# TensorE multiplies a constant matrix, into banks that nobody reads, while it waits in the opening and at the changes of stage

## The chip, the cores and the metric

One core of one Trainium2 chip runs the whole program. The metric is the device time of one execution in microseconds; less is better. TensorE has two clock levels, 1.2 and 2.4 GHz; the profile shows the granted level of each stretch as 0.50 or 1.00.

## The reference, cut to what matters

Two layers, each a gated cross attention and a gated mixture of experts, over x (8 batches of 100 tokens of 512) and a context (8 batches of 722 rows of 512):

```python
x = x + tanh(g_xattn[0]) * perceiver_attention(ctx, layernorm(x), mask)      # 16 heads, keys = 722 context rows + 100 latents
x = x + tanh(g_ffn[0])   * experts(layernorm(x), 4 experts, best 2)
x = x + tanh(g_xattn[1]) * strided_attention(layernorm(x), ctx, stride 16)   # 16 heads, 45 keys each
x = x + tanh(g_ffn[1])   * experts(layernorm(x), 8 experts, best 2)
```

## The kernel before

The program runs four stages one after the other, each with a block for every engine and a barrier of all engines between them. Names in the profile carry the stage's letter: `a_` perceiver attention (0 to 985 us), `f_` the first expert stage (to 1510), `g_` the strided attention (to 1650; `ahead_` and `sums_` name tensors that it shares with stage f), `m_` the second expert stage (to the end). Instructions of one engine are issued in the order in which they are written, and semaphores tie the engines together; no planner reorders anything.

**Stage a, opening.** VectorE normalises the first four batches of latents (line 1051). TensorE turns them (`turn_latents(0)`, line 843), and then makes the queries of all heads in sixteen units (`queries(u)`, line 703): four fp32 products of 128x400 each, which the profile counts as eight instructions a unit. The first unit waits for the weights `wq_sb` from DRAM. ScalarE and VectorE split each unit into a high and a low part (lines 540 and 946), split the weights (586 and 1026) and the context rows (533 and 935). `keys(0, 0)` waits for fifteen low parts of the queries and for the split context, the first scores (line 759) for the low part of the first keys (line 951), which stands behind four splits of `wv` (line 1026) in VectorE's order.

**Stage a, end.** After the last attention, TensorE routes batch 6 (`route_next(B - 2)`, line 822), waits for VectorE to normalise batch 7 (line 1014), turns it (`turn_next(B - 1)`, line 807), waits for ScalarE to move it (line 575), and routes it. VectorE keeps the logits (line 1021), SyncE waits for its last stores, and the barrier follows.

**Expert stages, opening.** On POOL: constants. TensorE multiplies them into an index vector (lines 1643, 1644), and when VectorE has chosen the experts (line 1782), counts the tokens of each (1648, 1649). VectorE computes from the counts which token goes to which row, some 35 small operations. When it has written the expert of each slot (line 1813), TensorE's sequencer reads the first six of them into registers (`expert_of`, line 1653, `EARLY` = 6). When VectorE has written `at_row` (line 1836, two halves), sixteen products (line 1662) gather the row numbers. The sequencer reads the other expert numbers (eight in f, ten in m) meanwhile. VectorE, which has split four weight pieces in the meantime (line 1843), takes the row numbers over (line 1849); POOL starts the gathers (line 1548); when the first has landed, VectorE goes on with the other splits, the low parts of the tokens (line 1857) and the gates (lines 1903 to 1909), and TensorE turns the tokens (`turn_tokens`, line 1674) and makes the first hidden layer (`hidden`, lines 1161 to 1163).

**Stage g, opening.** TensorE projects four pieces of the context (`context(c)`, line 2358), each when it has landed, and turns the tokens (`tokens(b)`, line 2366) as VectorE normalises them (line 2516); then queries, for which the weights must be split.

Of the kernel before, what the change touches and what calls it, by code (L numbers as in the profile page):

```python
# [58 lines left out]
def perceiver_attention(nc, ctx_rows, ctx_cols, x_in, keep_mask, ln_cols, wq, wkv, wout,  # L59
# [7 lines left out]
    P = 128  # L67
# [29 lines left out]
    with ExitStack() as ctx:  # L97
# [54 lines left out]
        ident = sb("ident", [P, P])  # L152
        stats = sb("stats", [P, CT + 2, 6])
        mean_var = sb("mean_var", [P, CT + 2, 2])
        unread = sb("unread", [P, 2 * B + 2])
# [17 lines left out]
        kv_ps = ps("kv_ps", [P, 2, BANK])  # L173
        s_ps = ps("s_ps", [P, 2, 2 * BANK])
        t_ps = ps("t_ps", [P, BANK])
# [16 lines left out]
        const_done = sem("const_done")  # L192
# [16 lines left out]
        l_norm_done = sem("l_norm_done")  # L209
# [469 lines left out]
        def _(pe):  # L679
# [14 lines left out]
            def queries(u):  # L694
                h, m = divmod(u, PAIRS)
                pe.wait_ge(lat_t_done, KD * (h + 1))
                pe.wait_ge(wq_loaded, 16)
                if Q_RING[u][0] == "s":
                    pe.wait_ge(lat_t_done, 2 * KD)
                if q_before(u) is not None:  # L700
                    pe.wait_ge(q_lo_done, q_before(u) + 1)
                for k in range(KD):
                    ins = nc.tensor.matmul(q_bank(u)[:, 0:HM], wq_sb[:, k, P * m:P * m + P], lat_t[:, k, HM * h:HM * h + HM], start=(k == 0), stop=(k == KD - 1))
                ins.then_inc(q_ready, 1)
# [105 lines left out]
            def route_next(b):  # L810
                if b == 0:
                    pe.wait_ge(ahead.loaded, 16 * ahead.loads)
                if b == B - 1:
                    wait_read(pe, ("turn", b))
                else:
                    pe.wait_ge(o_free, o_use["turn", b] + 1)
                if b >= B - 2:
                    wait_kv("route", b)
                else:
                    wait_o("route", b)  # L820
                for k in range(KD):
                    ins = nc.tensor.matmul(route_bank(b)[0:M, 0:ahead.experts], xn_t[:, k, :], ahead.r_t[:, k, :], start=(k == 0), stop=(k == KD - 1))
                ins.then_inc(routed, 1)
# [12 lines left out]
            def turn_latents(h):  # L836
                pe.wait_ge(l_norm_done, HB * (h + 1))
                for k in range(KD):
                    u = KD * h + k
                    if u >= 4:  # L840
                        pe.wait_ge(lat_t_done, u - 3)
                    for j in range(HB):
                        ins = nc.tensor.transpose(l_bank(u)[:, M * j:M * j + M], lat[0:M, HB * h + j, P * k:P * k + P], ident[0:M, 0:M])
                    ins.then_inc(l_tr_done, 1)

            pe.wait_ge(const_done, 3)
            turn_latents(0)
            queries(0)
            queries(1)
            turn_latents(1)  # L850
# [40 lines left out]
            attend(n)  # L891
            finish_last(7)
            route_next(B - 2)
            turn_next(B - 1)
            route_next(B - 1)

        @block.vector
        def _(dve):
# [309 lines left out]
def gated_experts(nc, name, x_in, routing, pieces, gate, gates, y_pairs, x_out, core, tensors=None, ahead=None, handed=None):  # L1208
# [29 lines left out]
    with ExitStack() as ctx:  # L1238
# [400 lines left out]

        @block.tensor  # L1640
        def _(pe):
            pe.wait_ge(const_done, 5)
            nc.tensor.matmul(banks[:, CONST, 0:P], ones, earlier, start=True, stop=True)
            nc.tensor.matmul(banks[:, CONST, P:P + 1], earlier, ones[:, 0:1], start=True, stop=True).then_inc(iota_ready, 1)

            pe.wait_ge(chosen_done, 1)
            flat = "p b e -> p (b e)"
            nc.tensor.matmul(banks[:, POS, B * E:2 * B * E], ones[0:M, :], chosen[0:M, :, :].rearrange(flat), start=True, stop=True).then_inc(count_ready, 1)
            nc.tensor.matmul(banks[0:M, POS, 0:B * E], earlier[0:M, 0:M], chosen[0:M, :, :].rearrange(flat), start=True, stop=True).then_inc(count_ready, 1)
            pe.wait_ge(expert_done, 1)  # L1650

            def expert_of(n):
                return pe.value_load(expert[0:1, n:n + 1], min_val=0, max_val=E - 1)
# [2 lines left out]
                return [expert_of(FIRST[q] + s) for s in range(SIZE[q])]  # L1656

            slot_expert = [expert_of(s) for s in range(EARLY)]
            for i in range(B * TOP):
                if i % B == 0:  # L1660
                    pe.wait_ge(at_row_done, i // B + 1)
                ins = nc.tensor.matmul(banks[:, CONST, 0:2 * SLOTS], at_row[0:M, i, :], in_slot[0:M, i, :, :].rearrange("p t s -> p (t s)"),  # L1662
                                       start=(i == 0), stop=(i == B * TOP - 1))
            ins.then_inc(rows_ready, 1)
            slot_expert += [expert_of(s) for s in range(EARLY, CORE)]

            pe.wait_ge(const_done, 12)

# [81 lines left out]

            first_group(0, True, slot_expert)
            other_groups(0, slot_expert)
            pe.wait_ge(expert_done, 2)
            used = pe.value_load(expert[0:1, SLOTS:SLOTS + 1], min_val=0, max_val=SLOTS)
            with pe.If(used > CORE):
# [279 lines left out]
def strided_attention(nc, x_in, y_pairs, gates, ahead, sums, wq_t, bias_qkv, wo_t, bo, gate, x_out, routing):  # L2035
# [22 lines left out]
    with ExitStack() as ctx:  # L2058
# [285 lines left out]
        def _(pe):  # L2344
# [34 lines left out]
            def half(h):  # L2379
                for b in range(HB * h, HB * h + HB):  # L2380
                    pe.wait_ge(fill_free("x", b), bank_use["x", b] // 4 + 1)
                for n in range(KD * h, KD * h + KD):
                    queries(n)

            context(0)
            pe.wait_ge(const_done, 3)
            for b in range(HB):
                tokens(b)
            context(1)
            pe.wait_ge(wq_lo_done, KD)  # L2390
            half(0)
# [329 lines left out]
```

## Time and profile before

| | us |
|---|---|
| median of 3 runs | 2014.9 (2014.32 to 2020.66) |
| the profiled execution, its own time | 2010.7 |
| its span, first to last instruction | 2009.0 |
| TensorE busy | 1886.8 (94% of the span) |
| VectorE, ScalarE, POOL busy | 1006.6, 858.4, 639.8 |
| mean granted clock of TensorE | 0.971 |

Times in the rows below are counted from the start of the span. A row of TensorE's busy time says how long matmuls were in flight; an fp32 product is two instructions, an fp32r product or a turning one.

### The profile page before, as it was taken

How to read it: one execution, taken by the hardware profiler on the slowest of the kernel's cores; microseconds unless marked ns; L12 is line 12 of the kernel's file. 1: busy time of each engine (PE TensorE's matmuls, PEld its weight loads, DVE VectorE, ACT ScalarE, POOL GpSimd, SP SyncE). 2: the span in 40 equal slices, each digit the busy share in tenths (PEclk: the TensorE clock that was granted, in tenths of full speed). 3: DMA queues.
4: the chain of work that ended last, by engine and by line, in shares of the span. 5: the costliest groups of instructions: out<-in, count | busy, mean ns of one | idle time of the engine just before them, and what ended most of it. 6: DMA issues, size and time to landing. Idle time of an engine off the chain costs nothing. (4 is left out here: it accounts for less than half of the span.)

```text
span 2009.0 us, 35165 instructions
## 1 busy us (share of the span) xinstructions
PE 1886.8 (94%) x12136; PEld 1539.5 (77%) x12136; DVE 1006.6 (50%) x2225; ACT 858.4 (43%) x1796; POOL 639.8 (32%) x519
## 2 busy tenths in 40 slices
PE   6999999999999999999599999999997876999994
PEld 3688787887878787878478888888884766999984
DVE  5526564655555554535553333233345657544565
ACT  3334453544444444435443334233323535655650
POOL 1230201102030302000045554355521204787882
PEclk9999999999999999999789999999998987999997
DMA  8840112121121211000343333133358035645546
GB/s 234 302 135 23 55 39 81 39 81 39 55 64 55 63 41 42 9 27 13 108 121 110 111 115 125 46 111 111 119 202 306 9 98 181 193 154 168 209 147 216
DMA packets 105398, 218.84 MB, mean 109 GB/s; under 512 B 25295, under 2 KB 26095, under 8 KB 103323
## 3 DMA queue, kind: packets, MB, share of 16 engines
q1 hardware_dynamic: 100451, 201.21, 31.2%
q0 software_dynamic: 4800, 15.73, 2.3%
q8 instruction: 85, 1.39, 0.3%
q14 instruction: 62, 0.51, 0.1%
HBM read 188.46 MB, written 28.04 MB: 108 GB/s over the span
## 5 line engine op out<-in xcount | busy, mean ns | idle before, releaser
L501 POOL TENSOR_TENSOR a_kvin_raw<-a_kvin_raw,a_rows 128x722 f32<-128x722 f32 x32 | 57.0, 1782 | 555.9 <-DMA a_rows<-a_norm_dram 555.9
L682 PE MATMUL a_kv_ps<-a_kvin_hi,a_wk_hi 128*128 128x512 f32 (+1 forms) x512 | 190.4, 372 | 0.0
L1161 PE MATMUL f_banks<-f_wab_hi,f_x_hi 128*128 x448 | 183.8, 410 | 1.1 <-DVE f_x_lo L1857 1.1
L684 PE MATMUL a_kv_ps<-a_kvin_hi,a_wk_lo 128*128 128x512 f32 (+1 forms) x512 | 179.7, 351 | 0.0
L683 PE MATMUL a_kv_ps<-a_kvin_lo,a_wk_hi 128*128 128x512 f32 (+1 forms) x512 | 178.9, 350 | 0.0
L1163 PE MATMUL f_banks<-f_wab_hi,f_x_lo 128*128 x448 | 176.8, 395 | 0.0
L1162 PE MATMUL f_banks<-f_wab_lo,f_x_hi 128*128 x448 | 176.2, 393 | 0.0
L1602 ACT ACTIVATE f_h_sb<-f_banks 128x256 f32<-128x256 f32 x112 | 43.1, 385 | 292.9 <-PE f_banks L1163 292.9
L1879 DVE TENSOR_TENSOR f_h_sb<-f_h_sb,f_banks 128x256 f32<-128x256 f32 x112 | 47.2, 422 | 240.8 <-ACT f_h_sb L1602 239.4
L569 ACT ACTIVATE a_probs_t<-a_t_ps 128x500 f32<-128x500 f32 x128 | 74.9, 585 | 190.8 <-PE a_t_ps L773 190.8
L1161 PE MATMUL m_banks<-m_wab_hi,m_x_hi 128*128 x512 | 154.0, 301 | 1.6 <-DVE m_x_lo L1857 0.9
L682 PE MATMUL a_kv_ps<-a_wv_hi,a_kvin_hi 128*128 128x512 f32 (+1 forms) x384 | 152.3, 397 | 0.0
L684 PE MATMUL a_kv_ps<-a_wv_hi,a_kvin_lo 128*128 128x512 f32 (+1 forms) x384 | 151.8, 395 | 0.0
L579 ACT ACTIVATE a_probs<-a_probs,a_neg_max 100x822 f32<-100x822 f32 x128 | 125.4, 979 | 61.3 <-DVE a_neg_max L958 61.2
L683 PE MATMUL a_kv_ps<-a_wv_lo,a_kvin_hi 128*128 128x512 f32 (+1 forms) x384 | 151.5, 394 | 0.0
L1163 PE MATMUL m_banks<-m_wab_hi,m_x_lo 128*128 x512 | 145.4, 284 | 0.0
L1162 PE MATMUL m_banks<-m_wab_lo,m_x_hi 128*128 x512 | 145.0, 283 | 0.0
L958 DVE CUSTOM_DVE_ANT_0 a_probs<-a_s_ps,a_mask_add 100x822 f32<-100x822 f32 x128 | 128.6, 1004 | 1.4 <-PE a_s_ps L759 1.2
L1540 POOL TENSOR_TENSOR f_wy_lo<-f_raw,f_wy_hi 128x512 fp32r<-128x512 f32 x60 | 77.3, 1289 | 157.7 <-ACT f_wy_hi L1579 157.7
L562 ACT ACTIVATE a_k_hi<-a_kv_ps 128x512 fp32r<-128x512 f32 (+1 forms) x128 | 65.6, 514 | 105.6 <-PE a_kv_ps L684 105.6
L551 ACT ACTIVATE a_v_sb<-a_kv_ps 128x512 f32<-128x512 f32 x96 | 57.1, 595 | 123.6 <-PE a_kv_ps L684 123.6
L1540 POOL TENSOR_TENSOR m_wab_lo<-m_wab_raw,m_wab_hi 128x512 fp32r<-128x512 f32 x84 | 108.2, 1328 | 0.0
(423 smaller groups left out, 4791.8 us busy)
## 6 DMA issues: line engine op xcount, KB each, us to landing
f_raw<-f_pieces SPq DMA_DIRECT2D x94, 256.0 KB, 2.6
m_raw<-m_pieces SPq DMA_DIRECT2D x92, 256.0 KB, 3.0
f_wab_raw<-f_pieces SPq DMA_DIRECT2D x42, 512.0 KB, 5.9
m_wab_raw<-m_pieces SPq DMA_DIRECT2D x42, 512.0 KB, 6.0
a_kvin_raw<-a_ctx_t SPq DMA_DIRECT2D x8, 1444.0 KB, 8.1
a_rows<-ctx SPq DMA_DIRECT2D x8, 1440.0 KB
a_rows<-a_norm_dram SPq DMA_DIRECT2D x8, 722.0 KB, 5.4
ahead_piece<-g_ctx SPq DMA_DIRECT2D x2, 2880.0 KB, 19.9
```

Of the source, the lines that this page charges most:

```text
L551: nc.scalar.activation(v_sb[0:n, half, t, :], kv_bank("v", i, v)[0:n, 0:HALF], ACT.Copy).then_inc(kv_sem("v", i, v), 1)
L562: nc.scalar.activation(k_hi[:, c:c + w], kv_bank("k", n, part)[:, 0:w], ACT.Copy).then_inc(k_hi_done, 1)
L569: nc.scalar.activation(probs_t[:, x, M * a:M * b], turned_bank(x, 0), ACT.Copy).then_inc(ta_done, 1)
L579: nc.scalar.activation(probs[0:M, x, 0:KEYS], probs[0:M, x, 0:KEYS], ACT.Exp, scale=-1.0, bias=neg_max[0:M, x:x + 1], accum_out=row_sum[0: ...
L682: nc.tensor.matmul(out, hi_l, hi_r, start=first, stop=False)
L683: nc.tensor.matmul(out, hi_l, lo_r, start=False, stop=False)
L684: return nc.tensor.matmul(out, lo_l, hi_r, start=False, stop=last)
L958: nc.vector.tensor_tensor_reduce(out=probs[0:M, x, 0:KEYS], in0=s_ps[0:M, x, 0:KEYS], in1=mask_add[0:M, :], scale=-1.0, scalar=3.0e38, op0 ...
L1161: nc.tensor.matmul(out, left_hi, right_hi, start=start, stop=False)
L1162: nc.tensor.matmul(out, left_hi, right_lo, start=False, stop=False)
L1163: return nc.tensor.matmul(out, left_lo, right_hi, start=False, stop=stop)
L1540: nc.gpsimd.tensor_tensor(split_dst(wab_lo, wy_lo, c), raw_of(q, n), split_dst(wab_hi, wy_hi, c).bitcast(F32), ALU.subtract).then_inc(wlo_ ...
```

## The change

119 products are added to TensorE's stream. Each multiplies a 128x128 fp32 constant (the identity, or a matrix of ones in the expert stages) by itself into a PSUM bank whose content nobody reads. They carry no semaphore. Nothing is removed or moved; three waits are added ahead of products in places where TensorE would have waited a little later anyhow (for the first latents, for the first normalised batch, and for POOL's constants).

In numbers: 27 in the opening of a, 13 at its end, 30 in the opening of f, 4 at its end, 15 in the opening of g, 30 in the opening of m.

```diff
+            def unread(n, bank):
+                for _ in range(n):
+                    nc.tensor.matmul(bank[:, 0:P], ident[:, :], ident[:, :], start=True, stop=True)
+
             pe.wait_ge(const_done, 3)
+            unread(10, kv_ps[:, 0, :])
+            pe.wait_ge(l_loaded[0], 16)
+            unread(12, kv_ps[:, 0, :])
+            pe.wait_ge(l_norm_done, 1)
+            unread(2, kv_ps[:, 0, :])
             turn_latents(0)
+            unread(3, kv_ps[:, 0, :])
             queries(0)
...
             finish_last(7)
             route_next(B - 2)
+            unread(9, t_ps)
             turn_next(B - 1)
+            unread(2, t_ps)
             route_next(B - 1)
+            unread(2, t_ps)
...
+            def unread(n, of):
+                for _ in range(n):
+                    nc.tensor.matmul(banks[:, HT_T, 0:P], of, of, start=True, stop=True)
+
+            pe.wait_ge(const_done, 3)
+            unread(1, ones)
             pe.wait_ge(const_done, 5)
             nc.tensor.matmul(banks[:, CONST, 0:P], ones, earlier, start=True, stop=True)
             nc.tensor.matmul(banks[:, CONST, P:P + 1], earlier, ones[:, 0:1], start=True, stop=True).then_inc(iota_ready, 1)
+            unread(2, ones)
...
             nc.tensor.matmul(banks[0:M, POS, 0:B * E], earlier[0:M, 0:M], chosen[0:M, :, :].rearrange(flat), start=True, stop=True).then_inc(count_ready, 1)
+            unread(10, ones)
             pe.wait_ge(expert_done, 1)
...
             slot_expert = [expert_of(s) for s in range(EARLY)]
+            unread(11, ones)
             for i in range(B * TOP):
...
             slot_expert += [expert_of(s) for s in range(EARLY, CORE)]
+            unread(6, ones)
...
             other_groups(0, slot_expert)
+            if x_out is None:
+                unread(4, ident[:, :])
...
             context(0)
             pe.wait_ge(const_done, 3)
+            unread(10)
             for b in range(HB):
                 tokens(b)
+                if b == 1:
+                    unread(5)
             context(1)
```

## Rows read from the trace of the kernel before

**Rows 1.** The span and TensorE's mean granted clock, by core.
```profile
core 0: 2009.0 us, clock 0.971
```

**Rows 2.** Stretches: length, busy time of PE, PEld, DVE, ACT, POOL; granted clock; DMA share; GB/s.
```profile
78.70:976.70 898.00, 895.83 (x6418) 717.27 (x6416) 468.32 (x1065) 396.91 (x715) 111.50 (x65) 1.00 0.18 55
...
989.40:997.40 8.00, 0.00 (x0) 0.00 (x0) 7.21 (x30) 6.87 (x12) 0.00 (x0) 0.50 1.02 378
...
1018.40:1507.30 488.90, 488.88 (x2255) 398.03 (x2254) 170.65 (x349) 174.85 (x409) 231.19 (x187) 1.00 0.34 114
...
1577.90:1588.60 10.70, 8.29 (x80) 7.27 (x80) 8.76 (x12) 5.31 (x11) 4.72 (x4) 0.84 0.01 2
```

**Rows 3.** Timeline of TensorE in the opening: start, duration, engine, line, count, idle before.
```profile
22.64 5.67 PE L703 MATMUL a_t_ps<-a_lat_t,a_wq_sb 128*128 128x400 f32 x8 [4.84 <-DMA a_wq_sb<-L_xattn_Wq]
28.11 2.98 PE L703 MATMUL a_o_ps<-a_lat_t,a_wq_sb 128*128 128x400 f32 x8
...
77.39 0.47 PE L759 MATMUL a_s_ps<-a_k_hi,a_q_hi 64*100 64x512 f32 x2 [2.77 <-DVE a_k_lo L951]
```

**Rows 4.** Timeline of VectorE ahead of the first scores.
```profile
68.82 0.56 DVE L946 SCALAR_TENSOR_TENSOR a_qs_lo<-a_kv_ps,a_qs_hi 128x400 fp32r<-128x400 f32 x1
...
71.62 4.63 DVE L1026 TENSOR_TENSOR a_wv_lo<-a_wout_sb,a_wv_hi 128x1024 fp32r<-128x1024 f32 x4 [0.37 <-ACT a_wv_hi L586]
```

**Rows 5.** Timeline of TensorE at the end of stage a.
```profile
975.88 0.79 PE L822 MATMUL a_kv_ps<-f_ahead_r_t,a_xn_t 128*100 128x4 f32 x8
981.31 0.93 PE L807 MATMUL a_kv_ps<-a_ident,a_res 100*128 100x100 f32 x4 [4.64 <-DVE a_res L1014]
982.83 1.49 PE L822 MATMUL a_kv_ps<-f_ahead_r_t,a_xn_t 128*100 128x4 f32 x8 [0.59 <-ACT a_xn_t L575]
```

**Rows 6.** SyncE's waits, 960 to 990 us: total, times, longest.
```profile
SPq L480 <- DMA f_xn<-a_res: 2.2, 1, 2.2
```

**Rows 7.** Timelines of SyncE's queue and of VectorE at the end of stage a.
```profile
981.28 0.27 SPq L403 DMA_DIRECT2D f_xn<-a_res  x1
...
984.36 0.16 DVE L1021 TENSOR_TENSOR logits<-a_kv_ps,f_ahead_r_bias 100x4 f32<-100x4 f32 x1 [3.11 <-PE a_kv_ps L822]
```

**Rows 8.** Register loads of TensorE's sequencer, f: duration ns min/median/max, first and last start.
```profile
L1653 PEldq SEQ_ASSERT  x6: 18/18/28, 993.5 to 996.7; - x6
...
L1653 PEldq TENSOR_LOAD <-f_expert x8: 295/300/308, 998.6 to 1003.1; - x8
```

**Rows 9.** The same in stage m, first six.
```profile
L1653 PEldq SEQ_ASSERT  x6: 18/18/18, 1660.9 to 1664.2; - x6
```

**Rows 10.** Timeline of TensorE in the opening of f.
```profile
986.89 0.80 PE L1643 MATMUL f_banks<-f_scratch 128*128 128x128 f32 x2 [2.56 <-POOL f_scratch L1528]
...
997.46 3.60 PE L1662 MATMUL f_banks<-f_in_slot,f_at_row 100*128 100x32 f32 x16 [8.07 <-DVE f_at_row L1836]
...
1018.42 0.49 PE L1161 MATMUL f_banks<-f_wab_hi,f_x_hi 128*128 x1
```

**Rows 11.** Timeline of VectorE in the opening of f.
```profile
998.46 2.49 DVE L1843 TENSOR_TENSOR f_wab_lo<-f_y_acc,f_wab_hi 128x512 fp32r<-128x512 f32 x4
...
1005.28 2.54 DVE L1843 TENSOR_TENSOR f_wab_lo<-f_y_acc,f_wab_hi 128x512 fp32r<-128x512 f32 x4 [3.67 <-DMA f_y_acc<-f_xn,f_rows_at]
...
1017.39 0.68 DVE L1857 TENSOR_TENSOR f_x_lo<-f_banks,f_x_hi 128x512 fp32r<-128x512 f32 x1
```

**Rows 12.** The chain of work that ended last, in the opening of m.
```profile
1665.64 3.62 PE m_banks L1662 x16
...
1669.73 3.26 DMA m_y_acc<-m_xn,m_rows_at
```

**Rows 13.** Timeline of TensorE in the opening of g.
```profile
1510.58 5.03 PE L2358 MATMUL g_banks<-ahead_piece,ahead_wk 128*32 128x360 f32 x32 [3.30 <-PEq L2657]
...
1523.66 1.57 PE L2366 MATMUL g_banks<-g_ident,sums_y_got 100*128 100x100 f32 x8 [5.08 <-DVE sums_y_got L2516]
...
1546.01 2.63 PE L2358 MATMUL g_banks<-ahead_piece,ahead_wk 128*32 128x360 f32 x32 [0.64 <-DMA ahead_piece<-g_ctx]
```

More of the change, by code:

```diff
@@ L2383, in half, with unread @@
                     queries(n)
+            def unread(n):
+                for _ in range(n):
+                    nc.tensor.matmul(banks[:, Y, 0:P], ident[:, :], ident[:, :], start=True, stop=True)
             context(0)
             pe.wait_ge(const_done, 3)
+            unread(10)
             for b in range(HB):
                 tokens(b)
+                if b == 1:
+                    unread(5)
             context(1)
```

## The prediction

> **What bounds the kernel now.** I read four views in this order. The clock by core comes first [rows 1]: 0.971 over 2009.0 us. With two levels, 1.00 and 0.50, that is (1 - 0.971) x 2009.0 / 0.5 = 117 us at the low one. The table of stretches says where not: in the long middle of stage a and in nearly all of f, TensorE is busy for 895.83 of 898.00 us and for 488.88 of 488.90, at 1.00 [rows 2]. There TensorE is the bound, and a microsecond that a stage's opening gains or loses goes through to the end. The low level lies at the changes of stage, and there TensorE mostly waits: in 989.4 to 997.4 it is busy for 0.00 us, and VectorE for 7.21 [rows 2]. The timelines then show what ends each wait, and what is late next; in the openings it is a DMA or VectorE. In the opening I go by durations: the same eight instructions take 5.67 us at 22.64 and 2.98 at 28.11 [rows 3]. The first unit ran at the low level.
>
> So the change can only gain where TensorE's work at the low level ends last, and it can lose where a filler stands in front of real work that is ready.
>
> **What one filler costs.** It is an fp32 product of 128 columns, two instructions. The query units have 400 columns: (28.11 - 22.64) / 4 = 1.37 us a product at the low level, 2.69 / 4 = 0.67 at the full one (2.98 less the 0.3 in which the last one drains) [rows 3]. By columns, 128 / 400 of that is 0.44 and 0.21 us. The nearest row of the form itself is 0.80 us for one product at the low level, from start to drained [rows 10]; behind one another they overlap, so I take 0.43 and 0.21, and 0.15 more for the first of a sequence.
>
> **Opening of a (27 fillers).** They end before what they stand in front of. The last three follow the turned latents, some 18 us, and take 1.3 us at most; the queries start at 22.64, when their weights land [rows 3]. So they cost nothing, and 3.5 to 5.5 us without work remain ahead of the queries. In this trace the level was low after 4.64 us of idling [rows 5], after 3.30 and after 5.08 [rows 13], and still full after 2.77 (two 64x512 products in 0.47) [rows 3]. I take the low level, gain 0. The other bound: with the first unit at full level TensorE is 2.7 us ahead. But the fifteenth low part of the queries is done at 68.82 + 0.56 = 69.4 whatever TensorE does, since VectorE is then working through a queue; the sixteenth then ends near 69.9 and not at 71.25, and the four splits, 4.63 us, and the keys' low part, which end the wait of 2.77 at 77.39, can start 1.7 us earlier [rows 3, 4]. Gain 0 to 1.7.
>
> **End of a (13).** Nine fillers fill 1.9 of the 4.64 us ahead of the turning [rows 5], leaving 2.7; by the same rows the level rather holds. Then turning ends 0.4 us earlier, routing takes 0.79 instead of 1.49, together 1.1 [rows 5]. The barrier needs the store as well: SyncE has issued it at 981.55 and waits 2.2 us, so to 983.75, while VectorE's last operation ends at 984.52 [rows 6, 7]. Gain 0.75. If the level is low, the two fillers behind the last routing (0.85 us) end at 984.32 + 0.85 = 985.2, a loss of 0.65. I take the gain.
>
> **Openings of f and m (30 each).** Here I expect the sum to be made. Three fillers go around the constants; two of them can hold the counts up for 0.4 us at the low level. I take 0, because VectorE has other small operations to do ahead of reading the counts, and keep 0.4 as the bound. Ten follow the counts at 989.4 and run to 991.5 or 993.8. The six register loads follow when VectorE has written the experts, one each 0.64 us, and end at 996.7 [rows 8]. They are the sequencer's, and the eight further ones from 998.6 run beside the sixteen products that end at 1001.06 [rows 8, 10], so loads and products don't wait for each other, only for their turn in the stream. The eleven fillers thus start at 996.7, and the sixteen products behind them, which started at 997.46, must wait for all eleven. TensorE has idled for 3 to 5 us by then: low level, as above.
> - Low to the end: 996.7 + 0.15 + 11 x 0.43 = 1001.6, and 3.6 us of products [rows 10] end at 1005.2 instead of 1001.06: 4.1 late.
> - Lifted on the way, at the soonest: in the rows the level rose 5.5 us after work began at 22.64 [rows 3]; the shortest low spell in stage g, with TensorE at work through most of it, lasted 10.70 x (1 - 0.84) / 0.5 = 3.4 us [rows 2], and I take that as the lower bound. Then eight fillers are low and three full: 996.85 + 3.4 + 0.65 = 1000.9, the sixteen at half their time 1.8, to 1002.7: 1.6 late.
> - Full from the start: 996.85 + 2.3 + 1.8 = 1000.95, no gain, since VectorE splits until 1000.95 and only then takes the rows over [rows 11].
>
> I take the middle of the first two, 2.9. Nothing hides it: the gathers wait for those rows, VectorE for the gathers (1005.28), and from there its queue runs to the low part at 1017.39 to 1018.07 that lets TensorE go on at 1018.42 [rows 10, 11]. For the same reason what the full level gives to the turning and first hidden layers in between (some 3 us of TensorE) is worth nothing. The last six fillers start near 1003.8 and end by 1006.5, before the shifted landing at 1006.9 or later.
>
> In m the loads end at 1664.2 and the sixteen started at 1665.64 [rows 9, 12]. Low to the end: 1664.2 + 0.15 + 4.7 + 3.6 = 1672.7 instead of 1669.26, 3.4 late. Lifted: 1664.35 + 3.4 + 0.65 + 1.8 = 1670.2, 0.9 late. Full: nothing. I take 2.2. The six last fillers start near 1673.2, after the landing at 1673.0 [rows 12]; at the low level they hold the tokens for up to 2.5 us, of which the first four splits (2.5 us) and the shift hide most: 0 to 1, I take 0.
>
> A rule of the Trainium skill speaks against this part too: "TensorE: Matmul & The Clock Gate", What happens when you issue a matmul, has weight loads pulled ahead of matmuls in flight, and the matmuls themselves kept in program order. By it the eleven can't be overtaken, which is the 1.6 to 4.1 above; if the queue let ready products pass, f and m would cost 0. No row of before shows either, since no ready product stands behind another there.
>
> **End of f and opening of g (4 and 15).** The four take 1.0 us of the 3.30 to the barrier [rows 13]. In g, ten end before 1523.66 even at the low level, and five (2.2 us) go into a later wait for VectorE's tokens; were they a few tenths late, the third piece would hide it. What the full level could give (some 4 us on two pieces of context) ends at the third piece: TensorE waits for its DMA at 1546.01 already [rows 13]. Zero, both ways, but for a shift of a few tenths.
>
> **The sum.** 0 - 0.75 + 2.9 + 2.2 = +4.35 us on 2010.7, the profiled execution's own time (1.7 above its span): 2015.0. The median of the runs, 2014.9, is 4.2 above that execution; the same shift makes 2019.2.
>
> **The rivals.** *Kept level:* the fillers do hold the clock at 1.00, at least at the eleven. Against: 3 to 5 us of idling that the loads force. For: 21 of the fillers lie within 12 us. Then f and m cost nothing: -0.75, and -1.7 with the opening: 2012.5 to 2014.2, and 2013.8 as its centre. It ends on the other side; the point that decides is the duration of the first of the eleven, 0.43 or 0.21. *One late:* one of f and m lifts or keeps, the other doesn't: about +1.5, 2016.5. *All of it paid:* TensorE's work at the low level is on the path after all, and half of its time comes back: 2.7 + 1.1 in a, 1.8 and some 3 in f, 2.5 (of 5.03) and some 2 in g, 1.8 and some 2 in m [rows 3, 5, 10, 12, 13], 17 us: 1998. Against: every wait that I followed there ends in VectorE or a DMA. A rule would make even more of it: the page named above, under Terms, puts the penalty at the throttled time times one minus the level; by it the sum would be 117 x 0.5 = 58 us less. The trace does not agree: TensorE was busy in 0.00 of the 8.00 us of one such stretch. *Nothing happens:* the fillers change neither level nor rows; within 0.5 us of 2014.9.
>
> **How the numbers follow.** Late rows in f and m: 0.55. One late: 0.13. Kept: 0.14. All paid, or much of it: 0.08. Nothing: 0.10. The low bound takes in the kept level, 2012.0. The high one is both losses in full, 4.1 + 3.4 - 0.75 and the last six, +7.5: 2022.5. What a measurement of this kernel can tell from no change is 0.3%, 6 us. The likeliest case passes it only at its upper end, about a third of the time: slower 0.20, faster 0.09, within 0.71.
>
> **What would show it.** The sixteen products start near 1001 instead of 997.5 and last 1.8 to 3.6 us; VectorE waits for them and takes the rows over 1.6 to 4.1 us later, and likewise in m. The queries at 22.64 still take 5.5 us. At the end of a the turning lasts 0.5 and the barrier comes 0.75 earlier. It would be wrong if the eleven took 0.21 each, or if the six register loads no longer ended at 996.7, since then the gap ahead of the sixteen moves.

## The result, and the profile after

The changed kernel took 2023.9 us (median of 14 runs, 2019.9 to 2030.6), the kernel before 2016.0 us beside it (median of 14, 2012.3 to 2020.7): ratio 1.0037, 95% interval 1.0027 to 1.0047, so 5.4 to 9.5 us slower. The forecast was 2019.2 us, within 2012.0 to 2022.5: the sign of the sum was right, its size too small, and the time lies outside the range. The profiled execution took 2019.9 us, span 2018.1, 9.1 more than the span before.

Clock of the one core, the counterpart of [rows 1]:

```profile
core 0: 2018.1 us, clock 0.974
```

The clock rose, from 0.971 to 0.974, and the kernel became slower. The rise isn't only this execution's. Averaged over their runs, six of the seven kernels of the experiments with fillers in the openings of both f and m lie 0.002 to 0.004 above the kernel before beside them (0.969 to 0.972 against 0.966 to 0.968); the three with fillers in a alone lie at 0.966 to 0.967, no higher than before. So the fillers of the expert stages do raise the clock a little, and what they buy was not on the path. TensorE in the opening of f, the counterpart of [rows 10] (start, duration, line, count, idle before and what ended it):

```profile
988.25 4.61 PE L1657 MATMUL f_banks<-f_scratch 128*128 128x128 f32 x20
995.67 4.01 PE L1657 MATMUL f_banks<-f_scratch 128*128 128x128 f32 x22 [2.80 <-issue]
999.33 2.38 PE L1684 MATMUL f_banks<-f_in_slot,f_at_row 100*128 100x32 f32 x16
1004.19 2.92 PE L1657 MATMUL f_banks<-f_scratch 128*128 128x128 f32 x12 [2.49 <-issue]
1006.91 1.13 PE L1697 MATMUL f_banks<-f_ident,f_y_acc 128*128 128x128 f32 x8
```

Line 1657 is the filler; two instructions are one filler. The third row is what VectorE waits for (1.92 us, until 1001.74). The same place in m:

```profile
1660.14 4.58 PE L1657 MATMUL m_banks<-m_scratch 128*128 128x128 f32 x20
1668.08 4.90 PE L1657 MATMUL m_banks<-m_scratch 128*128 128x128 f32 x22 [3.35 <-issue]
1672.73 1.94 PE L1684 MATMUL m_banks<-m_in_slot,m_at_row 100*128 100x40 f32 x16
1678.97 2.93 PE L1657 MATMUL m_banks<-m_scratch 128*128 128x128 f32 x12 [4.29 <-issue]
1681.69 1.65 PE L1697 MATMUL m_banks<-m_ident,m_y_acc 128*128 128x128 f32 x8
```

The fourth and fifth rows are the place that I had taken for free: the turning starts when the six fillers are through, not when the tokens land (1678.43, the next fence's first row), and VectorE then has nothing to do for 2.45 us:

```profile
1678.43 2.54 DVE L1868 TENSOR_TENSOR m_wab_lo<-m_y_acc,m_wab_hi 128x512 fp32r<-128x512 f32 x4 [3.19 <-DMA m_y_acc<-m_xn,m_rows_at]
1683.42 0.69 DVE L1882 TENSOR_TENSOR m_x_lo<-m_banks,m_x_hi 128x512 fp32r<-128x512 f32 x1 [2.45 <-ACT m_x_hi L1602]
```

Before, with the same columns, it had no gap at all between the two, and the turning stood 0.29 us behind the landing. The third row is ScalarE's high part, on which the low part waits:

```profile
1673.01 2.54 DVE L1843 TENSOR_TENSOR m_wab_lo<-m_y_acc,m_wab_hi 128x512 fp32r<-128x512 f32 x4 [3.21 <-DMA m_y_acc<-m_xn,m_rows_at]
1673.30 2.29 PE L1674 MATMUL m_banks<-m_ident,m_y_acc 128*128 128x128 f32 x8 [4.06 <-DMA m_y_acc<-m_xn,m_rows_at]
1674.42 0.60 ACT L1589 ACTIVATE m_x_hi<-m_banks 128x512 fp32r<-128x512 f32 x1 [6.21 <-PE m_banks L1674]
1675.47 0.68 DVE L1857 TENSOR_TENSOR m_x_lo<-m_banks,m_x_hi 128x512 fp32r<-128x512 f32 x1
```

TensorE's waits in the changed kernel, 975 to 2018 us (total, times, longest):

```profile
PE m_banks L1711 <- DVE m_h_sb L1904: 8.1, 5, 4.0
PE m_banks L1657 <- issue: 7.6, 2, 4.3
...
PE f_banks L1657 <- issue: 5.3, 2, 2.8
```

"Issue" ahead of a filler is the register loads: nothing that the fillers waited for, but what stood ahead of them in the stream. The first row is the longest wait behind the opening of m: TensorE waits up to 4.0 us for VectorE, where it waited 2.4.

Since single executions differ by chance (see the last section), I read every trace by stretches between two events that only the work between them can move. Worked out from the timelines, in us:

| stretch | before | after | difference |
|---|---|---|---|
| start to the first scores of a | 77.39 | 76.89 | -0.50 |
| to the barrier of f | 908.50 | 907.87 | -0.63 |
| to VectorE taking over the rows in f | 15.21 | 16.98 | +1.77 |
| to the last product of f | 505.79 | 505.80 | 0.01 |
| to SyncE's first load of y in g | 5.06 | 6.38 | +1.32 |
| to the third piece of context | 34.06 | 35.56 | +1.50 |
| to the constants' product in m | 106.53 | 106.88 | +0.35 |
| to VectorE taking over the rows in m | 16.74 | 18.35 | +1.61 |
| to the first gated `h_sb` of m | 15.04 | 17.52 | +2.48 |
| to the end | 324.68 | 325.87 | +1.19 |

### The profile page after: what moved, and what is told of

It is laid out like the page before. It is cut to its first block and busy times, and to the rows that moved or that the text cites. A ratio compares the mean times of both kernels' runs of the same rounds, so it can differ in the third digit from the quotient of the medians.

```text
span 2018.1 us, 35639 instructions
## 1 busy us (share of the span) xinstructions
PE 1919.9 (95%) x12374; PEld 1574.6 (78%) x12374; DVE 1006.4 (50%) x2225; ACT 858.5 (43%) x1796; POOL 640.0 (32%) x519
```

## The experiments

Twelve kernels in four groups, each group timed beside the kernel before on one chip: medians of before 2015.7 (experiments 1 to 4), 2016.6 (5 to 8), 2025.4 (9 to 11), 2015.1 (12). Differences are ratio minus one, times 2016, with the 95% interval. An interval is some 6 us wide, wider than most questions asked; the medians say how much a kernel costs in all, the stretches of the traces say where. There is one trace of each kernel, fourteen with the two above. "Landing" is the time from which the first gathered tokens are there, read from the start of VectorE's split that waits for them; "rows" is the time at which VectorE takes the row numbers over; "the sixteen" are the products that gather them.

### 1. Without the eleven

```diff
             slot_expert = [expert_of(s) for s in range(EARLY)]
-            unread(11, ones)
             for i in range(B * TOP):
```

> The changed kernel without the eleven unread products ahead of the sixteen row products, in both expert stages; all other fillers stay. Theory (queueing): in f and m nothing but the register loads stands ahead of the sixteen products, so they start within 0.5 us of VectorE's first half of at_row, as before the change, and VectorE takes the rows over when its own four splits are done: 1.8 us earlier than in the changed kernel in f, 1.6 us in m. Of the +7.5 us of the medians about +4 remain, because the six fillers behind the second register loads still hold the tokens of m for 2.4 us. Rival (the eleven are the whole price, as my sum had it): the time falls back to the kernel before, within 1 us.

Ratio 1.0033 (1.0020 to 1.0045): +6.7 us (4.0 to 9.1). In the trace VectorE takes the rows over 14.97 us behind the barrier of f and 16.74 behind the constants of m: 2.0 and 1.6 us less than in the changed kernel, to the hundredth the time of before in m. The sixteen wait for `at_row` again, and the six still hold the tokens:

```profile
1671.08 3.60 PE L1683 MATMUL m_banks<-m_in_slot,m_at_row 100*128 100x40 f32 x16 [4.74 <-DVE m_at_row L1860]
1678.67 2.92 PE L1657 MATMUL m_banks<-m_scratch 128*128 128x128 f32 x12 [4.00 <-issue]
1681.39 1.91 PE L1696 MATMUL m_banks<-m_ident,m_y_acc 128*128 128x128 f32 x8
```

The rival, that the eleven are the whole price, falls. But I had expected about +4 to remain, and the median fell by 0.8 us only, from +7.5 to +6.7; the interval just reaches down to 4.0. That the eleven cost 1.6 to 2.0 us a stage is read from the stretches; the times alone don't show it.

### 2. Without the six, in m alone

```diff
-            unread(6, ones)
+            if x_out is None:
+                unread(6, ones)
```

> The changed kernel without the six unread products behind the second register loads, in stage m alone. Theory: the loads of the ten expert numbers end after the tokens have landed, the six fillers stand behind the loads and the turning of the tokens behind the fillers; without them the turning starts at the end of the loads, VectorE's first low part of the tokens 2.5 us earlier against the landing, the later wait for m_h_sb shrinks from 4.0 us to about 2.4 and the group behind it stays at full level: 2.5 to 3.7 us less than the changed kernel, about +4 to +5 against the kernel before. Rival (VectorE's four splits cover the six, as predicted): the same time as the changed kernel, +7.5.

Ratio 1.0022 (1.0007 to 1.0037): +4.4 us (1.4 to 7.5), the profiled execution 3.2 below the changed kernel's. From the landing to the first gated `h_sb` 11.31 us, as before (11.31; changed kernel 13.80), and the wait behind it is 2.2 us instead of 4.0:

```profile
1679.43 2.16 PE L1698 MATMUL m_banks<-m_ident,m_y_acc 128*128 128x128 f32 x8 [4.35 <-DMA m_y_acc<-m_xn,m_rows_at]
```

```profile
PE m_banks L1712 <- DVE m_h_sb L1905: 6.3, 5, 2.2
```

That the splits cover the six, which I had predicted, is wrong. The times alone would not have told it, since the intervals of this kernel and of the changed one overlap; the stretch does.

### 3. The six ahead of the second loads

```diff
-            slot_expert += [expert_of(s) for s in range(EARLY, CORE)]
             unread(6, ones)
+            slot_expert += [expert_of(s) for s in range(EARLY, CORE)]
```

> The changed kernel with the six unread products moved ahead of the second register loads, in both expert stages: same number of fillers, other place. Theory (it is the place behind the loads that costs): they run directly behind the sixteen products while the sequencer reads the registers, and the tokens are turned at the end of the loads; the same gain as taking them out of m, 2.5 to 3.7 us below the changed kernel. Rival (the six cost wherever they stand, for example by moving the loads behind them): the ten loads start later by the time of six products, 1.3 to 2.6 us, and nothing is gained.

Ratio 1.0037 (1.0023 to 1.0051): +7.5 us. Half of each theory: the turning starts 2.02 us behind the landing (changed kernel 3.26, without the six 0.46), and the stretch to `h_sb` takes 12.58 us (13.80 and 11.31).

```profile
1675.34 1.94 PE L1684 MATMUL m_banks<-m_in_slot,m_at_row 100*128 100x40 f32 x16
1677.12 1.59 PE L1657 MATMUL m_banks<-m_scratch 128*128 128x128 f32 x12
1683.03 1.94 PE L1697 MATMUL m_banks<-m_ident,m_y_acc 128*128 128x128 f32 x8 [4.32 <-issue]
```

The ten loads ran from 1676.5 to 1683.0. In the changed kernel they began 0.2 us ahead of the sixteen, here 1.2 us behind their start, when some 10 of the 16 were through, so that about 6 of them and the 12 instructions of the fillers were still to run. So fillers ahead of loads aren't free: they hold the loads up as soon as the sequencer is some 17 instructions ahead (see the last section).

### 4. Twelve instead of six, in m

```diff
-            unread(6, ones)
+            unread(6 if x_out is None else 12, ones)
```

> The changed kernel with twelve instead of six unread products behind the second register loads of m. Theory: each further filler delays the tokens by its own duration, 0.42 us at the low level and 0.21 at the full one; in the changed kernel the level rose while the six ran or just after, so six more cost 1.3 to 2.5 us: +9 to +10 against the kernel before, and the turning starts that much later behind the landing. Rival (hidden by VectorE's splits): unchanged, +7.5.

Ratio 1.0054 (1.0033 to 1.0074): +10.9 us (6.7 to 14.9), 3.4 above the changed kernel, where +1.3 to +2.5 was expected. The trace gives the dose:

```profile
1685.47 5.43 PE L1657 MATMUL m_banks<-m_scratch 128*128 128x128 f32 x24 [3.68 <-issue]
1690.73 1.04 PE L1697 MATMUL m_banks<-m_ident,m_y_acc 128*128 128x128 f32 x8
```

Twelve take 5.43 us, six took 2.93; from the constants' product to the turning it is 27.84 us, against 25.33 with six and 22.66 with none: 2.7 us for the first six, 2.5 for the second. Behind the landing it shows less, 15.26 us to `h_sb` against 13.80, because the rows, and with them the landing, were 0.6 us later in this trace.

### 5, 6 and 9. One region at a time

The changed kernel with only the fillers of a (40), only those around the barrier between f and g (19), only those of the expert openings (60).

> Only the fillers of stage a (27 in the opening, 13 at its end); nothing is added in f, g and m. Theory: the end of a gains 0.6 us from its last attention to the barrier and nothing else changes: 2 us at most below the kernel before, within what can be told from no change. f, g and m then have the same durations from milestone to milestone as before the change, and g's first load of y is issued 5.1 us after the last product of f, not 5.7 to 6.6 as in the four runs with fillers there. Rival (the extra loss of 1.2 us at the head of g and the 1.5 us in the landing of its third piece are chance or come from elsewhere): the same 5.7 to 6.6 here.

> Only the four fillers at the end of f and the fifteen in the opening of g. Theory (as in the prediction, they lie beside DMAs): the first product of g comes 0.4 us later behind the last of f (4.07 instead of 3.69 us, which five traces showed), the rest nothing: within 1 us of the kernel before. Rival (the fillers at the end of f or in g cost what the changed kernel lost there in its profiled execution): +2.5 us, with the load of y issued 6 to 6.5 us behind the last product of f and the third piece 35.5 us behind that.

> Only the 30 fillers in the opening of f and the 30 in that of m; none in a, at the end of f and in g. Theory: these alone make the change slower. From the barrier to VectorE's taking over of the rows +1.4 to +2.4 us in f (0.34 of them ahead of the counts) and +1.6 in m, from the landing in m to the first gated h_sb +2.5, and up to 1.2 behind it: +6 to +7.5 us in all, and the load of y in g issued 4.4 to 5.3 us behind the last product of f, as in the five traces without this pair of places together. Rival (the fillers around f's end and in g are needed for the loss, though alone they cost nothing): +4 or less.

| kept | ratio | us |
|---|---|---|
| a | 1.0000 (0.9985 to 1.0014) | 0 (-3 to +3) |
| end of f and g | 1.0000 (0.9986 to 1.0015) | 0 (-3 to +3) |
| openings of f and m | 1.0027 (1.0014 to 1.0040) | +5.4 (2.8 to 8.1) |

The loss is made in the expert openings; their interval reaches down to 2.8, so the times don't exclude the rival (that the nineteen are needed for a part of it, +4 or less). There, alone, barrier to rows took 16.99 us in f, constants to rows 18.27 in m, landing to turning 3.21: the changed kernel's numbers. From the landing to `h_sb` it was 16.12, more than the changed kernel's 13.80: VectorE idled 3.06 us ahead of it, where it idled 0.80 before, and ScalarE's `h_sb`, for which the profile names no wait, came late too. No filler stands there; the cause is open. The end of a didn't gain in experiment 5: from the sixth batch's routing to the barrier it took 10.36 us with its thirteen fillers, against 10.01 before. With the nineteen alone (experiment 6), the first product of g came 4.41 us behind the last of f (3.69 or 3.70 in all seven traces without them) and the third piece 39.94 us behind it (38.3 to 39.5 in those seven). Their interval of 3 us would hide the 2.5 of the rival; it is the trace that speaks against it, with the load of y 4.66 us behind the last product of f and not 6 to 6.5.

### 7. Ten behind the turned latents

```diff
             turn_latents(0)
-            unread(3, kv_ps[:, 0, :])
+            unread(10, kv_ps[:, 0, :])
             queries(0)
```

(f, g and m as before.)

> As the kernel with only the fillers of a, but ten instead of three of them behind the turned latents, so that TensorE's idling ahead of the queries is under 2 us instead of 3.8. Theory: the level rises on the way and holds, the first unit of queries takes 3.0 us instead of 5.4, and what follows is bounded as the prediction says: the first scores come up to 1.7 us earlier. Rival 1: the level falls again and the fillers, still at the low level, end behind the landing of the weights, so that the queries start up to 1 us late. Rival 2: the first unit is fast, but the first scores don't come earlier, as VectorE's queue ends last: 0.

Ratio 0.9993 (0.9977 to 1.0009). The ten ran at the full level, so they were over in 2.42 us, 3.97 us of idling remained, and the queries ran at the low one, 5.67 us, so that the first scores came 54.80 us behind their start, as before (54.75). My bridge was too short by my own price list: I had sized it at the low level.

### 8. The eleven ahead of the first loads, no six

```diff
-            unread(10, ones)
+            unread(21, ones)
             pe.wait_ge(expert_done, 1)
...
             slot_expert = [expert_of(s) for s in range(EARLY)]
-            unread(11, ones)
...
-            unread(6, ones)
```

(a as changed; nothing at the end of f and in g.)

> Expert stages with the eleven fillers moved ahead of the first six register loads (21 in a row behind the counts), the six behind the second loads left out; a as in the changed kernel, none at the end of f and in g. Theory: a sequencer runs only some 11 to 15 products ahead of its engine (in three traces the ten register loads of m began 2.0 to 2.5 us before the last product ahead of them ended), so the 21 push the loads by about 1.3 us in m, but the sixteen row products start at most 0.5 us later than VectorE's first half of at_row would let them: f and m cost 0 to 0.5 us each instead of 1.7 and 1.6 plus 2.5; the whole is -1.5 to +1 us against the kernel before. Rival (fillers delay by their own time wherever they stand in the queue): +1.6 in each of f and m, about +3 in all.

Ratio 0.9996 (0.9982 to 1.0010): -0.8 us. Barrier to rows in f 14.97 us (15.21 before), constants to rows in m 16.52 (16.74), landing to `h_sb` 11.31. Nothing unread stands in front of ready work any more:

```profile
1659.64 7.64 PE L1657 MATMUL m_banks<-m_scratch 128*128 128x128 f32 x42
1668.96 2.21 PE L1683 MATMUL m_banks<-m_in_slot,m_at_row 100*128 100x40 f32 x16 [1.68 <-DVE m_at_row L1857]
1676.68 2.05 PE L1695 MATMUL m_banks<-m_ident,m_y_acc 128*128 128x128 f32 x8 [5.51 <-DMA m_y_acc<-m_xn,m_rows_at]
```

The same 21 fillers, ahead of the loads instead of astride of them, cost nothing: the rival (their own time wherever they stand) falls. The expectation's "11 to 15 products ahead" was worked out from traces in which the sequencer had waited for `at_row`; where it hadn't, it is some 17 (experiment 3).

### 10. Nothing but the six of m

```diff
             slot_expert += [expert_of(s) for s in range(EARLY, CORE)]
+            if x_out is not None:
+                unread(6, ones)
```

> The kernel before with nothing but six unread products behind the ten register loads of m. Theory: the price of the place by itself. The loads end as the tokens land (0.3 us apart before the change), TensorE has idled for 4 us and the level is low: the turning starts 6 x 0.43 = 2.6 us later, and VectorE's first low part of the tokens comes 2.3 to 2.6 us later behind the landing, with nothing that makes up for it: +2.3 to +3.7 us. Rival (it needs the eleven before it, which push the loads): under 1 us.

Ratio 1.0012 (0.9997 to 1.0028): +2.4 us (-0.6 to +5.6); landing to turning 2.90 us (0.29 before), to the first low part of the tokens 4.62 (2.46): +2.16, to `h_sb` 13.97 (11.31): +2.66. Of the last, 0.43 is idling of VectorE just ahead of `h_sb` (1.23 us, 0.80 before) that no filler explains.

```profile
1676.08 2.93 PE L1648 MATMUL m_banks<-m_scratch 128*128 128x128 f32 x12 [3.98 <-issue]
1678.80 1.50 PE L1684 MATMUL m_banks<-m_ident,m_y_acc 128*128 128x128 f32 x8
```

Six products that nobody reads, alone, cost 2.2 to 2.7 us in this trace; the interval of the times still touches no change. It doesn't need the eleven.

### 11. The version that the stretches point to

Stage a alone, with 24 behind the turned latents and none behind the last routing.

```diff
             turn_latents(0)
-            unread(3, kv_ps[:, 0, :])
+            unread(24, kv_ps[:, 0, :])
...
             route_next(B - 1)
-            unread(2, t_ps)
```

> The version that the stretches point to: stage a alone, with 24 fillers instead of three behind the turned latents, and without the two behind the last routing. Theory: at the full level the 24 take 5.8 us and end within 1 us ahead of the weights' landing; then the first unit of queries takes 2.9 us, and as the first scores came 49.0 to 49.1 us plus the first unit's own duration behind its start in six traces, they come 1.5 to 2.7 us earlier than the 54.75 of before. The barrier comes 0 to 0.6 us earlier and never later, since nothing unread stands ahead of it. In all -1.5 to -3.3 us. Rival 1: the level is low while they run, they take 10 us, the queries start some 4 us late and the kernel is 2 to 4 us slower. Rival 2: VectorE's queue takes over as the bound at 1.3 us, the most that those six traces showed.

Ratio 0.9989 (0.9975 to 1.0003): -2.2 us (-5.0 to +0.6). In the trace:

```profile
16.70 7.10 PE L848 MATMUL a_kv_ps<-a_ident 128*128 128x128 f32 x48
23.64 2.85 PE L703 MATMUL a_t_ps<-a_lat_t,a_wq_sb 128*128 128x400 f32 x8
```

The first unit takes 2.85 us, and the first scores come at 75.48, 51.84 us behind its start (54.75 before); neither rival holds as it was put. Counted from the start of the program they are 1.9 us earlier, not 2.9, because the fillers took 7.10 us and not 5.8, and ended about 1.1 us behind the time at which the queries start elsewhere (22.1 to 22.8 in twelve traces, 23.59 in experiment 4). Some 20 of them might do better; that wasn't tried. The end of a took 10.01 us, as before. This is the fastest version tried, and its interval still touches no change.

### 12. Without the four at the end of f

```diff
-            if x_out is None:
-                unread(4, ident[:, :])
```

> The changed kernel without the four fillers at the end of f; all others stay. Five traces with all the places filled show SyncE's first load of y in g 5.7 to 6.6 us behind the last product of f, eight others, among them one with these four but without those of the expert openings, 4.35 to 5.3. Theory: the barrier comes 0.3 to 0.4 us earlier, as in every trace without the four, and no more is theirs: the load of y keeps 5.3 to 6.2 us. Rival: the four are behind the whole delay, and it falls to 4.35 to 5.3. Against the kernel before +5.5 to +7.5 us either way; the trace decides, not the median.

Ratio 1.0056 (1.0040 to 1.0073), from 6 runs: +11.3 us (8.1 to 14.7), more than the changed kernel and more than the 5.5 to 7.5 expected, which the edit does not explain. The one trace speaks against my theory: first product of g back to 3.70 us behind the last of f, the load of y at 5.23, within the rival's 4.35 to 5.3. So the delay of about 1.2 us goes with the four; but alone with those of g they left it at 4.66 (experiment 6). Why is open, and one trace of each kernel doesn't exclude chance. The trace also shows the eleven at the low level to the end:

```profile
1672.57 5.06 PE L1657 MATMUL m_banks<-m_scratch 128*128 128x128 f32 x22 [3.74 <-issue]
1677.28 3.58 PE L1684 MATMUL m_banks<-m_in_slot,m_at_row 100*128 100x40 f32 x16
```

## Why the prediction was wrong, point by point

**Price of a filler: right.** 4.90 / 11 = 0.45 and 4.58 / 10 = 0.46 us at the low level, 2.42 / 10 = 0.24 at the full one; predicted 0.43 and 0.21, and 0.15 for the first.

**Opening of a: gain 0, bound 1.7. VectorE's queue isn't as fixed as I had it.** In all fourteen traces the first scores come 49.0 to 49.2 us plus the duration of the first unit behind the queries' start. So what the unit gained arrived in full, 1.3 us in experiment 5 and 2.8 in experiment 11, where I had VectorE's queue cut the gain at 1.7. I had taken the fifteenth low part to be done at 69.4 whatever TensorE does; in experiment 11 it was done at 68.26. But there the queries started 1.0 us later than before, and in experiment 5, where they started at 22.44, VectorE worked without a gap right up to its splits, so nothing was left there. Whether more than 1.3 us would arrive with queries that start on time is not shown. That the changed kernel gains little is right for the other reason given: 3.80 us of idling ahead of the queries, which took 5.37 us (4.75 to 5.67 without the fillers, 4.33 to 5.57 with the 27).

**End of a: -0.75, bound +0.65. Both happen.** From the sixth routing to the barrier it was 10.01 or 10.02 us in four traces without the fillers. With the thirteen it was 9.41, 9.41 and 9.53 where the level held through the last routing, and 10.10 to 10.67 in the six others, where the two fillers behind it stood ahead of the barrier. The mean of the nine is 10.12, a loss of 0.1. The changed kernel's profile happened to be of the first kind:

```profile
980.78 0.56 PE L807 MATMUL a_kv_ps<-a_ident,a_res 100*128 100x100 f32 x4 [2.53 <-DVE a_res L1027]
981.94 0.87 PE L822 MATMUL a_kv_ps<-f_ahead_r_t,a_xn_t 128*100 128x4 f32 x8
```

**Opening of f, +2.9; of m, the eleven, +2.2: mechanism right, somewhat too large.** The loads end 10.91 us behind the barrier (10.81 predicted), the eleven start there and the sixteen behind them. Barrier to rows in f rose by 1.6 to 2.5 us in six traces; the two fillers ahead of the counts make TensorE 0.34 us later with them, but VectorE reads them 4.12 us behind the barrier in all fourteen traces, so they cost the 0 that I had put. Constants to rows in m by 1.5 to 1.6 in four traces, 2.2 in one and 3.3 in experiment 12, which is my "low to the end" (3.4). Experiments 1 and 8 remove it from the stretches.

The Trainium skill ("TensorE: Matmul & The Clock Gate", What happens when you issue a matmul) has matmuls keep program order; the traces agree: the turning started at 1681.69, behind the six, though its tokens had landed at 1678.43.

**The six of m, 0 (0 to 1): this step failed, it is +2.5.** The prediction said: "they hold the tokens for up to 2.5 us, of which the first four splits (2.5 us) and the shift hide most". The 2.5 us that they hold them was right (2.7). The cover was not: I set the delay against the length of the work beside it, and not against what was left of it. During those same four splits (2.46 us) the turning of the first tokens and ScalarE's high part have to be done as well, and they take 2.0 of it. The slack measured: 3.26 - 0.29 = 2.97 us more from the landing to the turning gave 2.53 more to the low part, so 0.44 us was hidden; 1.73 gave 1.32 (experiment 3), so 0.41. And the shift hides nothing, because the same fillers cause it: the ten loads moved with the rows (their end at 1673.1 before and 1678.97 after, the landing at 1673.01 and 1678.43).

In f the same six cost nothing in this trace: it has eight loads, not ten, and these ended 1.8 us ahead of the landing, so the turning was 0.95 us late and landing to low part stayed at 2.46 us. In other traces of f they cost up to 0.96.

**Behind the opening of m: 1.2 us here, which I can't put down to the fillers.** The two groups of TensorE behind the turning, now at the full level, are done sooner, VectorE is later, the wait becomes 4.0 instead of 2.4 us, and the group behind it runs at the low level, 0.21 us from product to product instead of the 0.12 of the group at 1684.48. From the first product of `h_sb` to the next it takes 4.24 us, where it took 2.86 before:

```profile
1692.58 0.33 PE L1711 MATMUL m_banks<-m_ident,m_h_sb 128*128 128x128 f32 x1 [3.99 <-DVE m_h_sb L1904]
...
1693.84 0.42 PE L1175 MATMUL m_banks<-m_wab_lo,m_x_hi 128*128 x1
1694.06 0.41 PE L1176 MATMUL m_banks<-m_wab_hi,m_x_lo 128*128 x1
```

That looks like a higher level earlier that bought a lower one later, and without the six (experiment 2) the group is back at 2.86 us and the stretch at 324.62. But the kernels of experiments 5, 6 and 7, which have no filler in m and waited 1.6 us there, show the same group at the low level, for 4.40 us each, and last stretches of 326.5 to 327.8 us; with the six and a wait of 2.5 us (experiment 1) it took 2.86. From experiment 5:

```profile
1683.17 0.33 PE L1705 MATMUL m_banks<-m_ident,m_h_sb 128*128 128x128 f32 x1 [1.59 <-DVE m_h_sb L1896]
...
1684.37 0.42 PE L1175 MATMUL m_banks<-m_wab_lo,m_x_hi 128*128 x1
1684.59 0.41 PE L1176 MATMUL m_banks<-m_wab_hi,m_x_lo 128*128 x1
```

So the level of this group differs between traces with and without fillers, and the 1.2 us are a difference between two executions until more of them are compared.

**End of f and opening of g, 0 and 0: +0.34 measured at the barrier, and 2.5 us more whose cause is open.** The first product of g comes 0.3 to 0.7 us later in all six traces that have the four: TensorE was not so early at the barrier that they fit in. From the last product of f to the third piece of g the seven traces without any of the nineteen took 38.3 to 39.5 us, the five with all fillers 40.2 to 41.9. Part is the later load of y (5.06 and 6.38), the rest the landing of the third piece, which TensorE's fillers do not touch. The load of y waits for f's last scatter to land. POOL issues that scatter 1.4 us behind the last product of f in all fourteen traces; SyncE then waits for it 1.6 to 2.3 us in the five with all fillers and at most 1.3 in the nine others. Before and in the changed kernel:

```profile
SPq L2180 <- DMA y<-f_y_acc,f_rows_at: 1.1, 1, 1.1
SPq L2205 <- DMA y<-f_y_acc,f_rows_at: 2.1, 1, 2.1
```

So it is a DMA that lands later though it is issued at the same time. That it goes with the fillers is shown, not why. Alone, the nineteen measured as 0, within 3 us either way (experiment 6).

**The sum.** Predicted -0.75 + 2.9 + 2.2 = +4.35. The trace has -1.13 in a, +1.77 and +1.61 for the rows, +2.48 for the six, +1.19 behind them, +3.17 between f's last product and m (1.32 + 1.50 + 0.35): +9.09, the difference of the spans. Traced to fillers are the rows and the six, 5.86 us together; the 60 fillers of the expert openings alone cost +5.4 (experiment 9). The 1.19 and the 3.17 are not traced to them. The ratio of the runs gives 5.4 to 9.5.

Had the six been entered at the 2.5 us for which they hold the tokens, the forecast would have been +6.85 and the high bound +9.25 (2024.2), just above the measured 2023.9. The bound as it stood is a little under its own terms (4.1 + 3.4 - 0.75 + 1 = 7.75, not 7.5), and its base of 2014.9, a median of three runs, was 1.1 us below the later median of fourteen. That the middle of the measured difference, +7.5, equals the bound is chance. The rivals *kept level*, *all of it paid* and *nothing* are excluded by the ratio; *one late* by the stretches.

## What to carry to other kernels

A filler in an in-order queue is free only if everything behind it is late anyway: ask what ends each wait, and put it ahead of what ends the wait, not behind. Sequencer work (here 0.64 us a register load) moves with the queue, and here the fillers that followed it landed just where the real work became ready; the same 21 fillers cost 0 ahead of the loads and 1.6 to 1.8 us a stage astride of them. And when a delay is to be "hidden" by work beside it, subtract first what already hides there: here 2.5 us of cover had 0.4 us left.

## What the runs showed of the hardware that I had not expected

**The level is not the program's alone.** The first unit of queries took 5.67, 4.75, 5.67 and 5.35 us in four kernels that have the same code up to there, and the thirteen fillers of a ended at either of two outcomes in nine. The eleven of m ran at the low level in the changed kernel and in experiment 12, behind 3.35 and 3.74 us of idling; the sixteen behind them then took 1.94 us in the one and 3.58 in the other. What a few fillers buy thus varied from trace to trace; that they cost something in front of ready work did not.

**How far the sequencer runs ahead.** In the changed kernel the second loads began at 1672.5, 0.2 us before the first of the sixteen, though `at_row` had been complete since 1670.5: the instructions ahead in the stream held them. In the four other traces with the eleven in place and no filler between the sixteen and the loads (experiments 2, 4, 9, 12) they began 0.2 to 0.3 us ahead of the first of the sixteen too. Where the sixteen had to wait for `at_row` (before, experiments 1, 8, 10), the loads began within 0.1 us of its second half. That, and experiment 3, put it at some 17 matmul instructions, an estimate worked out from these starts.

**Chance in single executions.** Stretches in which TensorE never waits for a filler differ between these kernels: first scores to barrier 907.9 to 910.6 us, f from its third low part to the last product 489.5 to 492.9, the last stretch of m 324.6 to 337.8, the longest on the chip whose runs of before had their median at 2025.4. So the difference of two spans, +9.1 here, can be off by several us, and only short stretches, repeated over traces, carry a term of 0.5 us.
